# Cross-attention with a mixture-of-experts block on one Trainium2 core: two heads to a score job, on 64-row halves of the TensorE array

## What is computed

```python
# x: 4 batches x 512 rows x 256; y (context): 4 x 1601 x 192; 16 heads of 16
q = (layernorm(x) @ Wq + bq).reshape(B, N, 16, 16)
k = (y @ Wk + bk).reshape(B, M, 16, 16)
v = (y @ Wv + bv).reshape(B, M, 16, 16)
attn = softmax(einsum('bnhd,bmhd->bhnm', q, k) / sqrt(16), axis=-1)
out = einsum('bhnm,bmhd->bnhd', attn, v).reshape(B, N, 256)
x = x + tanh(g_xattn) * (relu(out @ W1 + b1) @ W2 + b2)
# then: x = x + tanh(g_ffn) * (shared expert + 2 of 8 routed experts)(layernorm(x))
```

## Time and profile before

| | us |
|---|---|
| median of 3 runs | 1333.47 |
| lowest and highest | 1330.21, 1335.7 |
| span of the profiled execution | 1354.8 |
| PE busy in it | 1254.9 (93%) |
| DVE busy | 749.8 (55%) |
| ACT busy | 546.8 (40%) |

### The profile page before, as it was taken

How to read it: one execution, slowest core, us unless ns; L and a number is a source line. 1 busy time by engine, 2 the same in 40 slices (tenths; PEclk the granted TensorE clock), 3 DMA queues, 4 the chain that set the end, 5 groups by cost and what they waited for, 6 DMA issues and landing times. The chain is left out here.

```text
span 1354.8 us, 16247 instructions
## 1 busy us (share of the span) xinstructions
PE 1254.9 (93%) x5662; PEld 704.1 (52%) x5662; DVE 749.8 (55%) x1624; ACT 546.8 (40%) x1004; POOL 97.3 (7%) x114
## 2 busy tenths in 40 slices
PE   6899999999999999999999999997858999999982
PEld 2455545555645555554555565544434555555551
DVE  1498776686776588576668778632601222222244
ACT  1006564564555366346456547771201111111110
POOL 4000000000000000000000000000170000000044
PEclk9959999999999999899999999997988999999996
DMA  9344403323210453040322421010850111111124
GB/s 308 45 68 71 53 1 47 63 37 51 28 26 1 53 90 49 5 53 1 41 32 34 53 30 24 5 51 4 297 184 31 32 46 40 39 48 39 39 71 124
DMA packets 53840, 78.43 MB, mean 58 GB/s; under 512 B 13312, under 2 KB 38912, under 8 KB 53760
## 3 DMA queue, kind: packets, MB, share of 16 engines
q1 hardware_dynamic: 47744, 67.01, 24.9%
q0 software_dynamic: 3072, 8.39, 1.9%
q10 hardware_dynamic: 2944, 1.98, 0.5%
HBM read 32.47 MB, written 16.52 MB: 36 GB/s over the span
## 5 line engine op out<-in xcount | busy, mean ns | idle before, releaser
L442 ACT ACTIVATE probs<-st_ps 128x512 f32<-128x512 f32 (+1 forms) x832 | 450.5, 598 | 361.8 <-PE st_ps L542 360.6
L677 DVE TENSOR_REDUCE mpart<-ring 128x1 f32<-128x402 f32 x1024 | 521.3, 568 | 85.0 <-PE ring L488 83.0
L488 PE MATMUL ring<-kst,qst 128*128 128x402 f32 x1024 | 389.1, 406 | 0.8 <-DVE xnT L637 0.3
L542 PE MATMUL st_ps<-qst,kst 128*128 128x512 f32 (+1 forms) x832 | 327.7, 400 | 1.9 <-ACT probs L442 1.8
L488 PEld LDWEIGHTS ring<-kst,qst 128*128 128x128 f32 x1024 | 200.1, 196 | 215.1 <-DVE mpart L677 175.9
L554 PE MATMUL pv_ps<-probs,vp 128*17 128x512 f32 (+1 forms) x1664 | 219.6, 600 | 0.1
L542 PEld LDWEIGHTS st_ps<-qst,kst 128*128 128x128 f32 (+1 forms) x832 | 154.0, 187 | 41.8 <-ACT probs L442 19.5
L845 ACT ACTIVATE s_sb<-gu_ps 128x512 f32<-128x512 f32 x55 | 32.9, 598 | 304.8 <-PE gu_ps L920 252.5
L920 PE MATMUL gu_ps<-wgu,xbT 128*128 x312 | 144.1, 604 | 7.4 <-issue 7.3
L1049 DVE TENSOR_TENSOR h_sb<-s_sb,gu_ps 128x512 f32<-128x512 f32 x55 | 37.8, 687 | 204.0 <-ACT s_sb L845 184.0
L920 PEld LDWEIGHTS gu_ps<-wgu,xbT 128*128 128x128 f32 x312 | 56.1, 189 | 78.5 <-issue 78.5
(11 more groups left out here) (125 smaller groups left out, 716.2 us busy)
## 6 DMA issues: line engine op xcount, KB each, us to landing
kst<-parts SPq DMA_DIRECT2D x192, 100.2 KB
qst<-parts SPq DMA_DIRECT2D x192, 32.0 KB
sorted_x<-zeros SPq DMA_DIRECT2D x1, 4992.0 KB, 16.4
xb<-sorted_x SPq DMA_DIRECT2D x39, 128.0 KB, 2.1
sorted_y<-ysb SPq DMA_DIRECT2D x39, 128.0 KB, 1.7
wgu<-in_WgT SPq DMA_DIRECT2D x16, 256.0 KB, 6.7
wgu<-in_WuT SPq DMA_DIRECT2D x16, 256.0 KB, 7.1
wd<-in_WdT SPq DMA_DIRECT2D x8, 512.0 KB, 8.4
```

Of the source, the lines that this page charges most:

```text
L442: nc.scalar.activation(probs[0:w, m % NPB, h, :], st_ps[0:w, (4 * m + h) % NST, :], ACT.Exp, scale=SCALE).then_inc(exp_done, 1)
L488: last = nc.tensor.matmul(slot[:, 0:SCH], qst[u % NKB][:, h, t * P:(t + 1) * P], kst[u % NKB][:, h // 2, score_at(q):score_at(q) + SCH], s ...
L542: nc.tensor.matmul(st_ps[0:w, idx % NST, :], kst[u % NKB][:, h // 2, mt * P:mt * P + w], qst[u % NKB][:, h, :], start=True, stop=True).the ...
L677: last = nc.vector.tensor_reduce(mpart[:, h, t, q:q + 1], slot[:, 0:SCH], AX.X, ALU.max)
```

## The change

Both halves of the array are now used one by one. An S job (line 501 in the changed file) is a pair of heads: two matmuls, the first on the partitions 0 to 47, the second on 64 to 111, into the two banks of one slot. One DVE instruction takes both maxima (128 x 2 x 402). An st (line 560) likewise uses 49 rows, from partition 0 or 64. The zeros in qst are no longer needed: qst keeps two heads side by side, [P, 2, N] instead of [P, 4, N], its memsets on POOL go, and so do the four zero-row DMAs of each unit (28 DMAs become 24).

A ring slot has two banks and there are NSLOT = 2 of them. Other jobs grow to two banks: Q is one job instead of two, K 4 instead of 8, V 4 instead of 7, XT and XT2 one instead of two, W1 two instead of four, W2 one instead of two. Their places in the steps change with that. The relu of W1 moves from DVE to ACT (two activations, released by a semaphore of its own, ring_free_act). Within a step PE's order is now S pair, st, st, S pair, st, st, the third S pair if there is one, pv, then the other jobs. A unit has 32 S pairs: three in six of 13 steps and two in seven. NST stays 3.

```diff
-NSLOT = 4
+NSLOT = 2
...
             if hg == 1:
-                extra[3], extra[5], extra[6] = qj[0:2], qj[2:3], qj[3:4]
-                for n in range(5):
-                    extra[8 + n] = k[n:n + 1]
+                extra[4], extra[7], extra[9], extra[11] = qj[0:1], qj[1:2], k[0:1], k[1:2]
             if hg == 2:
-                extra[0] = k[5:6]
-                extra[1], extra[3] = extra[1] + k[6:7], k[7:8]
+                extra[3], extra[5] = k[2:3], k[3:4]
                 for n in range(VJOBS):
-                    extra[4 + n] = v[n:n + 1]
+                    extra[6 + 2 * n] = v[n:n + 1]
...
-        ring = ctx.enter_context(nc.psum_tensor("ring", [P, NSLOT, 512], F32))
+        ring = ctx.enter_context(nc.psum_tensor("ring", [P, NSLOT, 2, 512], F32))
...
+                elif kind == "K":
+                    _, b, dt, g = job
+                    act.wait_ge(ring_full, count(job))
+                    nc.scalar.activation(kc[:, dt, 0, 2 * g * KCH:2 * (g + 1) * KCH].rearrange("p (i n) -> p i n", i=2),
+                                         slot[:, :, 0:KCH], ACT.Identity, bias=bk[:, dt:dt + 1]).then_inc(hi_ready, 1)
+                elif kind == "W1":
+                    g = job[2]
+                    act.wait_ge(ring_full, count(job))
+                    for i in range(2):
+                        f = 2 * g + i
+                        last = nc.scalar.activation(h1[:, f, :], slot[:, i], ACT.Relu, bias=b1[:, f:f + 1])
+                    last.then_inc(ring_free_act, 1)
...
+                    for j in range(2):
+                        rows = slice(64 * j, 64 * j + STK)
+                        last = nc.tensor.matmul(slot[:, j, 0:SCH], qst[u % NKB][rows, p, t * P:(t + 1) * P],
+                                                kst[u % NKB][rows, p, score_at(q):score_at(q) + SCH],
+                                                start=True, stop=True)
...
+                at = 64 * (h % 2)
+                rows = slice(at, at + STK + 1)
+                nc.tensor.matmul(st_ps[0:w, idx % NST, :], kst[u % NKB][rows, h // 2, mt * P:mt * P + w],
+                                 qst[u % NKB][rows, h // 2, :], start=True, stop=True).then_inc(st_full, 1)
...
+                for p in range(2):
+                    for job in chunks[p:p + 1]:
                         do(job)
-                    st(u, mt, h)
-                for job in chunks[4:] + others:
+                    for j in range(2):
+                        st(u, mt, 2 * p + j)
+                for job in chunks[2:]:
+                    do(job)
+                if MT * u + mt > 0:
+                    pv(MT * u + mt - 1)
+                for job in others:
                     do(job)
...
+                    nc.vector.tensor_reduce(mpart[:, 2 * p:2 * p + 2, t, q], slot[:, :, 0:SCH], AX.X, ALU.max
+                                            ).then_inc(ring_free, 1)
```

More of the change, by code:

```diff
@@ L128, in schedule @@
     b = B - 1
-    epilogue = ([("SUM", UNITS - 1), ("DIV", UNITS - 1)] + [("W1", b, f) for f in range(F1 // P)] +
-                [("W2", b, 0), ("W2", b, 1)])
+    epilogue = [("SUM", UNITS - 1), ("DIV", UNITS - 1), ("W1", b, 0), ("W1", b, 1), ("W2", b)]
     return prologue, steps, epilogue
@@ L189, in attention, with free_count @@
     leading = [job for job in order if job[0] in ("Q", "K")]
+    taken_by_act = [job for job in order if job[0] == "W1"]
+    taken_by_dve = [job for job in order if job[0] != "W1"]
+    place = {job: n for jobs in (leading,) for n, job in enumerate(jobs)}
+    freed = {job: n for jobs in (taken_by_act, taken_by_dve) for n, job in enumerate(jobs)}
     def hi_count(job):
-        return leading.index(job) + 1
+        return place[job] + 1
     def count(job):
         return slot_of[job] + 1
+    def free_count(job):
+        return freed[job] + 1
     with ExitStack() as ctx:
@@ L448, in _ @@
             take_pv(UNITS - 1)
+            for job in epilogue:
+                take_hi(job)
         @block.tensor
@@ L455, in do @@
                 if n >= NSLOT:
-                    pe.wait_ge(ring_free, n - NSLOT + 1)
+                    before = order[n - NSLOT]
+                    if before[0] == "W1":
+                        pe.wait_ge(ring_free_act, free_count(before))
+                    else:
+                        pe.wait_ge(ring_free, free_count(before))
                 kind = job[0]
                 if kind == "XT":
-                    _, b, dt = job
+                    b = job[1]
                     pe.wait_ge(xn_ready, NT * (b + 1))
-                    for t in range(NT):
-                        last = nc.tensor.transpose(slot[:, t * P:(t + 1) * P], xn[:, t, dt * P:(dt + 1) * P], ident[:])
+                    for dt in range(2):
+                        for t in range(NT):
+                            last = nc.tensor.transpose(slot[:, dt, t * P:(t + 1) * P], xn[:, t, dt * P:(dt + 1) * P],
+                                                       ident[:])
@@ L463, in do @@
                 elif kind == "Q":
-                    _, b, dt = job
-                    pe.wait_ge(ring_free, count(("XT", b, 1)))
-                    for k in range(2):
-                        last = nc.tensor.matmul(slot, wq[:, k, dt * P:(dt + 1) * P], xnT[:, k, :],
-                                                start=(k == 0), stop=(k == 1))
+                    b = job[1]
+                    pe.wait_ge(ring_free, free_count(("XT", b)))
+                    for dt in range(2):
+                        for k in range(2):
+                            last = nc.tensor.matmul(slot[:, dt], wq[:, k, dt * P:(dt + 1) * P], xnT[:, k, :],
+                                                    start=(k == 0), stop=(k == 1))
@@ L630, in do @@
                 kind = job[0]
-                if kind == "XT" and job[2] == 0:
+                if kind == "W1":
+                    return
+                if kind == "XT":
                     normalise(job[1])
```

224 lines of the change are left out of this document (99 added, 125 removed).

## The result

| | before | after |
|---|---|---|
| median, us | 1333.47 (5 runs, 1330.21 to 1336.71) | 1462.17 (5 runs, 1461.41 to 1486.29) |
| ratio after / before | | 1.099, 95% interval 1.093 to 1.106 |
| span of the profiled execution | 1354.8 | 1479.7 |
| loop, start of the first pv to start of the last | 815.3 | 955.6 |
| of it at a granted clock of 1.2 GHz | 17 | 354 |

The account below looks back on a forecast made before the run. It took a circle of waits through pv, st and exps to bound the plain step; -20.6 + 35 - 4.2 - 10 - 1.8 + 1.5 + 9 + 2 = +11 us on 1333.5 gave 1344 us, range 1315 to 1375.

Parts of the forecast that it names:

- the last term of the sum: Loop, behind K and Q jobs: idle time of TensorE lowers its clock, as after XT; +2 us.
- Rival 4: Clock falls behind the waits at 27 places (K, Q, V, W2): +30 us, 1374 us; chance 0.12.
- The overlap of the pairs: Plain step: a pair's two heads run side by side on the array halves, S pair to st 0.33 us.
- rival 3: Plain steps: the two halves run one after another, 2.9 us more a unit, +43 us, 1387 us; chance 0.10.
- The circle as the floor: Plain step: waits between pv, st and exps set 2.81 us, or 3.00 with three pairs; -20.6 us in all.
- rival 2: Plain steps: TensorE's work alone sets the step, VectorE then binds, 152 us less, about 1213 us; chance 0.04.
- The waits behind the ring: Steps after long jobs: second S pair waits for one of two slots; K +16, Q +5.7, V +3.7, W2 +5.7.
- W1 and XT: W1's relu +2.6 us, its DMA wait gone -10; XT's normalising mostly covered by pv, -4.2.
- The switches of the array: One more change of array arrangement at 84 ring jobs, 0.11 us each: +9 us, from 0 to 9.
- rival 1: Half arrays entered and left without the 0.11 us: circle 2.70, 1314 us, or about 1320 if half holds; chance 0.22.
- The last unit: Final 13 steps, without S: step of 2.59 us before, held by the circle of exp waits; change forecast 0.
- the rest of the sum but the clock: Terms beside plain steps: ring waits +35, XT -4.2, W1's DMA wait -10, prologue -1.8, epilogue +1.5, switches +9.

Follow-up runs that it names:

- a_full_rows: The changed kernel with every S and st again over all 128 rows, zeros in the other head's half; 1402.73 us, ratio 1.051.
- b_rows_only: The kernel before, with only S and st moved to the 48 or 49 rows of their own head, no pairs; 1333.46 us, ratio 0.999.
- k_plain_halves: a_full_rows with half rows in the 85 steps that neither hold nor follow a job other than S or MX; 1396.45 us, ratio 1.046.
- f_rows_fill: b_rows_only with one copy of the third st added in each step; 1390.47 us, ratio 1.040.
- e_fill_waits: c_fill with further copies of st, some 240, ahead of the second S pair in steps that follow a ring job; 1415.74 us.
- c_fill: The changed kernel with the third st of each step issued three times, 416 matmuls more; 1423.86 us.

## Why the prediction was wrong, point by point

- **The failed step is the last term of the sum**: "For idle time behind K and Q that lowers the clock, as after XT, +2". It measured at least +111, about +130 by the estimate above. The other terms came out together within a few us of their sum, so this one term is nearly the whole miss. Rival 4 named the right resource, but its price of 27 x 1.1 = +30 was taken from the earlier trace rows, where the pause was followed by one short stretch (3.4 us of half clock from 158.9 on). In the changed kernel a stretch lasts up to 37 us, because the plain steps behind it are on half rows too. Its reason was also incomplete: it blamed the pauses, and a_full_rows has pauses of 1.15 us at the same places at a clock of 0.99. I priced the clock by idle time and did not ask what it does when the matmuls themselves use 49 of 128 rows.
- **The overlap of the pairs** (rival 3 against it): right. S pair to st is 0.30, forecast 0.33.
- **The circle as the floor** (rival 2 against it): right, steps of 2.78 and 2.95 where 2.81 and 3.00 stood. The small difference is 8 us over 14.8 units, by which the change gains more than forecast.
- **The waits behind the ring**: right in place and size for K, V, Q and W2 (about +33 for +31.1).
- **W1 and XT**: right. The DMA wait is gone from the loop.
- **The switches of the array** (rival 1 against it): the jobs SUM, DIV and MX cost about 10 us where 6.5 was allowed; at full clock SUM adds 0.09 more to its step than before, MX 0.21 and DIV 0.36. Whether that is the switch or the ring is not separated. K, V and Q show none of it beyond their forecast, so of the +9 for 84 jobs no run shows the 4 us of the other 39. The Trainium skill (TensorEngine Tiling (Array Packing), Key Properties) speaks of a drain at each change of tiling mode; of its size these rows give a bound, no price.
- **The last unit**: forecast at nothing, about +4 at full clock; a step with XT2, now one job in place of two, takes 3.61 against 2.99, one with LG 4.48 against 3.90.
- **The 57 us of a_full_rows** agree with the working, though not to the microsecond: without the overlap the forecast's -20.6 turns into rival 3's +43 - 20.6 = +22, and 22 + 30 (the rest of the sum but the clock) is 52.

The order of sizes is worth a look: the halves save about 49 us at full clock on the new ring, the ring and the jobs of two banks cost 57, and the clock that is lost with both costs about 130. Undoing either part removes most of the last: a_full_rows has 14 us of half clock in the loop and takes 1403 us, b_rows_only has 76 and takes 1333. What it is in the halves that lowers the clock stays open.

## What to carry to other kernels

Before a matmul is moved to a part of the array, price the granted clock as a resource: the same instructions in the same order ran 1.6 times longer here (4.71 against 2.96 us), over 354 us. Use part of the array where TensorE has no pauses nearby, and full rows (zeros cost nothing but the lost overlap) around the steps in which it waits: on the old ring, halves in all steps were worth nothing (ratio 0.999), and halves in 138 of 208 steps 1.6%. On the new ring a like choice of steps (k_plain_halves) brought +9.9% down to +4.6%; the rest is the ring. And a step that is short of TensorE work by several tenths of a microsecond is not a free gain: adding 416 useless matmuls made the changed kernel 38 us faster.

## What the runs showed of the hardware

- A window 98% busy can have a granted clock of 0.50 for 71 us, beside one as busy at 1.00 (f_rows_fill). The first holds st on 49 rows, pv and a few short jobs; the second mostly S between them. The same unit of b_rows_only, 96% busy, ran at 1.00.
- Pauses of 1.15 us behind each K job leave the clock at 0.99 when the matmuls around them use all 128 rows (a_full_rows); with 48 or 49 rows half clock is 120 us even where the pauses are filled to 4.1 us for all twelve (e_fill_waits), and 354 where they are 1.75 us each (changed kernel).
- Matmuls that add nothing to the result made a kernel 38 us faster, through the clock: half clock in the loop fell from 354 to 191 us (c_fill).
- Two matmuls on different row halves overlap, in whatever order they are issued: an S pair passes in 0.30 us, and S beside the st of another head in b_rows_only brings the plain step from 3.02 to 2.77 us without any pairing in the code.
- A maximum over 2 x 402 columns in PSUM has a pitch of 0.91 us against 2 x 0.485: joining two saves 0.06 us.
